# GpSimd waits for its scatters to land before it ends its part of a block

## What is computed

```
x = x + 0.5 * ffn(layernorm(x))       # top-1 of 8 experts, silu(a) * g @ w2, times its probability
x = x + mamba(layernorm(x))           # conv, selective scan over 1024 steps, gate, out, layer norm
x = x + 0.5 * ffn(layernorm(x))
```

## Time and profile before

| | us |
|---|---|
| three runs | 426.71, 425.19, 426.67 |
| median | 426.67 |
| span of the profiled execution, first to last instruction | 421.5 |
| PE busy | 373.5 (89%) |
| DVE busy | 309.6 (73%) |
| ACT busy | 261.8 (62%) |
| GpSimd busy | 260.0 (62%) |

### The profile page before, as it was taken

The page is one execution under the profiler, slowest core; times in us unless marked ns, Lnnn a source line. Parts: engine busy times, 40 slices in busy tenths (PEclk is TensorE's granted clock), DMA queues, the critical chain, the costliest instruction groups (busy, mean ns, idle before and its releaser), DMA issues.

```text
span 421.5 us, 8456 instructions
## 1 busy us (share of the span) xinstructions
PE 373.5 (89%) x2962; PEld 339.5 (81%) x2962; DVE 309.6 (73%) x475; ACT 261.8 (62%) x508; POOL 260.0 (62%) x190
## 2 busy tenths in 40 slices
PE   7398999996799988999999899999998298999994
PEld 7297988896664377899998789999898297998994
DVE  2844454472699699999999999999979845544561
ACT  2314333341397999999999999999645414433330
POOL 7054666654001009999999999999960054666643
PEclk9679999999699999999999999999999689999999
DMA  6928592210300168654444344434337321121110
GB/s 197 346 61 253 131 406 64 47 33 32 101 0 4 30 165 20 150 158 132 126 158 155 125 126 166 144 130 130 108 117 285 90 40 41 38 47 46 40 39 25
DMA packets 42730, 47.47 MB, mean 113 GB/s; under 512 B 13313, under 2 KB 34370, under 8 KB 42178
## 3 DMA queue, kind: packets, MB, share of 16 engines
q1 hardware_dynamic: 37634, 39.72, 31.7%
q0 software_dynamic: 2944, 6.13, 6.1%
q10 hardware_dynamic: 2112, 1.08, 1.2%
HBM read 37.38 MB, written 9.54 MB: 111 GB/s over the span
## 4 chain that ended last, share of the span: by engine, by line
ACT 35%; PE 16%; DVE 15%; POOL 3%; issue 2%; another core or an unknown queue 1%; DMA 1%; POOLq 0%; DVEq 0%; ACTq 0%
ACT phase L1050 16%; ACT phase L1060 14%; PE psum L660 9%; PE psum L672 5%; DVE xc L1287 4%; DVE phase L966 3%; POOL w_sb L885 2%; DVE x_tok L1012 1%; ACT dt L920 1%; DVE xc L1283 1%; PE psum L1151 1%; PE psum L1183 1%; POOL phase L373 1%; DMA phase<-token_rows,token_row 1%
## 5 line engine op out<-in xcount | busy, mean ns | idle before, releaser
L885 POOL TENSOR_TENSOR w_sb<-phase,w_sb 128x1024 f32<-128x1024 f32 x62 | 144.7, 2378 | 0.0
L966 DVE TENSOR_TENSOR_SCAN phase<-phase,psum 128x1024 f32<-128x1024 f32 x64 | 142.1, 2272 | 3.0 <-PE psum L1133 2.3
L660 PE MATMUL psum<-phase 128*128 128x128 f32 x736 | 92.1, 277 | 4.6 <-ACT phase L559 2.9
L660 PEld LDWEIGHTS psum<-phase 128*128 128x128 f32 x736 | 86.5, 192 | 6.8 <-ACT phase L559 3.5
L373 POOL DMA_INDIRECT phase<-token_rows,token_row x46 | 47.2, 1027 | 55.3 <-DVE token_row L475 25.8
L1050 ACT ACTIVATE phase<-dtxT,B_cols 128x256 f32<-128x256 f32 x192 | 79.9, 495 | 0.2
L1151 PE MATMUL psum<-ident,w_sb 128*128 128x128 f32 x512 | 67.5, 276 | 3.3 <-DVE silu_z L959 0.9
L1060 ACT ACTIVATE phase<-dt,neg_A 128x1024 f32<-128x1024 f32 x64 | 69.6, 1136 | 0.0
L496 DVE TENSOR_TENSOR phase<-phase,psum 128x512 f32<-128x512 f32 x46 | 31.4, 684 | 45.1 <-PE psum L660 21.8
L1151 PEld LDWEIGHTS psum<-ident,w_sb 128*128 128x128 f32 x512 | 56.5, 141 | 8.7 <-POOL w_sb L885 6.9
L1124 PE MATMUL psum<-ident,phase 128*128 128x128 f32 x384 | 55.6, 276 | 1.5 <-DVE phase L966 0.6
(11 more groups left out here) (180 smaller groups left out, 401.5 us busy)
## 6 DMA issues: line engine op xcount, KB each, us to landing
w_sb<-c_rows SPq DMA_DIRECT2D x32, 512.0 KB, 3.9
w_sb<-ffn_w SPq DMA_DIRECT2D x16, 512.0 KB, 7.3
B_diag<-dt SPq DMA_DIRECT2D x4, 1024.0 KB
phase<-B_diag SPq DMA_DIRECT2D x32, 128.0 KB, 3.8
w_sb<-ffn_w SPq DMA_DIRECT2D x8, 256.0 KB, 7.8
token_rows<-x_tok SPq DMA_DIRECT2D x4, 264.0 KB, 4.9
token_rows<-x_tok ACTq DMA_DIRECT2D x4, 264.0 KB, 6.0
x_tok<-attn_x SPq DMA_DIRECT2D x4, 256.0 KB, 4.1
```

Source lines behind the costliest of these rows:

```text
L660: last = nc.tensor.matmul(psum[:, 2 * k + part, c * P:(c + 1) * P], w1_tile[:, t % W1_RING, part * F + c * P:part * F + (c + 1) * P], xsT_ ...
L885: nc.gpsimd.tensor_tensor(hC[:, k % HC_RING, :], H[:, k % H_RING, :], C_sb[:, j % C_RING, :], ALU.mult).then_inc(M["hC_ready"], 1)
L966: nc.vector.tensor_tensor_scan(H[:, k % H_RING, :], dA[:, k % DECAY_RING, :], dBx_bank[k % SLOTS], 0.0, ALU.mult, ALU.add).then_inc(M["sca ...
```

## The change

The function that waits for the scatters takes any engine, and GpSimd calls it behind its last scatter, in both expert layers. SyncE's own wait stays.

```diff
-        def wait_scattered(sp, f):
+        def wait_scattered(engine, f):
             for k in range(YS_RING):
-                sp.wait_ge(f["ys_stored"][k], f["ys_before"][k] + 16 * ((SLOT_TILES - 1 - k) // YS_RING + 1))
+                engine.wait_ge(f["ys_stored"][k], f["ys_before"][k] + 16 * ((SLOT_TILES - 1 - k) // YS_RING + 1))
...
                 scatter(t)
+            wait_scattered(pool, f)
```

## The result

The change makes the kernel slower: 428.84 us in the median of 8 runs (427.28 to 436.19) against 425.12 us in 8 runs of the kernel before (423.92 to 426.71). The ratio is 1.0067 with a 95% interval of 1.0036 to 1.0099, + 2.8 us by the ratio and + 3.7 us by the medians; forecast were + 3.3 us.

A forecast was written before the change was run, and what follows sets the result against it. TensorE was busy 89% of 421.5 us, but the change touches the block ends, where GpSimd's DRAIN sets the program's last 2.4 us. 1.57 + 1.75 = 3.3 us on 426.67 gives 430.0 us, range 424.4 to 431.0.

The forecast's parts named there:

- The DRAIN, started later: At both block ends: GpSimd's DRAIN, pushed behind the new waits, still takes 3.8 us as work of fixed length; chance 0.62.
- The rule that was weighed: At GpSimd's DRAIN: if it only waits for an idle engine, it would be over at once, giving 424.6 us.
- The turning point: At the program's end: a DRAIN under 2.2 us behind the wait would make the forecast wrong in sign.
- End of the program: At the second block's end: DRAIN ends at 422.8 in place of 421.25, nothing hides it, + 1.57 us.
- End of the first block: Release at 109.7 in place of 107.95, + 1.75 us, which the second block passes on in full.
- The starts that were named: Expected trace times: GpSimd's DRAIN at 105.7 (first block) and near 420.7 (program's end), VectorE's L820 near 109.8 us.
- TensorE's clock: Behind the first block's release: the clock's rise moves with the restart, the chain there runs through VectorE, so nothing added.
- The absolute time: Whole kernel: 426.67 us before plus 3.3 us gives 430.0 us.
- The reading of the 5.2 us: Outside the profiled span: the runs' median exceeds the span by 5.2 us, left as they are by the change.
- The first: Rival on GpSimd's DRAIN: it waits for outstanding DMAs and costs next to nothing once landed; 424.6 us, chance 0.17.
- the second: Rival on GpSimd's DRAIN: the 3.8 us start by themselves behind the last scatter, both releases stay; 426.7 us, chance 0.14.
- the third: Rival on the first block's end: its delay is taken up in the second block, + 1.57 us alone; 428.2 us, chance 0.07.

The follow-up runs named there:

- e5: Kernel before plus one GpSimd DRAIN inside each expert layer, behind tile 7 in the first and tile 15 in the second; one run for the trace, 424.75 us.
- e6: Kernel before plus a second GpSimd DRAIN right behind each layer's last scatter, ahead of the block's own; one run for the trace, 422.18 us.
- e8: Changed kernel, waits in both layers, plus an early GpSimd DRAIN behind tile 15 in both; ratio 0.9952 to the kernel before, 420.69 us.
- e7: Kernel before plus one early GpSimd DRAIN behind tile 15 of the second expert layer alone; ratio 0.9970, 421.59 us.
- e2: Changed kernel with GpSimd's wait in the first expert layer only; ratio 1.0033 to the kernel before, + 1.4 us.
- e1: Changed kernel with GpSimd's wait in the second expert layer only; ratio 1.0039 to the kernel before, + 1.7 us.

## Why the prediction was right

*The DRAIN, started later.* This step decided the sign, and held: 3.83 and 3.81 us behind the wait, 3.8 forecast. The reason given held in its first half (work of a length, begun when GpSimd gets to it, not a wait for data) and left open which work; e5, e6 and e8 showed it to be a price for each DMA issued since the last DRAIN. That it doesn't follow the landing is true only with many DMAs: with 7 to 24 of them it does, with half of its price still behind. Here there was luck in the argument. The two equal lengths in spite of unequal landings, on which it rested, came about because half of the price of 46 DMAs, 1.91 us, was just over the later landing, 1.80 us; with 40 DMAs the first block's DRAIN would have followed its landing by the fitted rule. The rule that was weighed, that a drain waits for the engine to be fully idle (the Trainium skill, "PSUM — Partial Sum Buffer", section "Engine vs sequencer instructions"), tells nothing of this price. The turning point that the prediction named, a DRAIN under 2.2 us behind the wait, holds only against a DRAIN that was long without the wait too. With few DMAs both are short, and the wait still costs: e8's takes 0.62 us behind the wait, and its end comes 2.45 us behind the last scatter, against 1.82 us in e7 without the wait.

*End of the program.* + 1.57 us forecast, 5.63 - 4.05 = 1.58 measured. The 0.15 us from wait to DRAIN, taken from SyncE, was right.

*End of the first block.* + 1.75 us forecast, 6.19 - 4.37 = 1.82 measured, and passed on: e2 alone costs 1.4 us of time (0.2 to 2.6). The starts that were named (105.7, 420.7, 109.8) came at 104.6, 422.7 and 108.75, because in this execution the stretch up to the first layer's last scatter took 1.1 us less and the one behind the release 3.0 us more; the distances from the last scatters are the ones forecast.

*TensorE's clock,* for which nothing was added. The profiled execution after does lose something there: in the stretch that was at 0.95 it is still at 0.50, 1.2 GHz, and its chain of waits runs through the preliminary tiles, 6.50 us for what took 5.79:

```profile
112.00:114.00 2.00, 2.00 (x11) 2.00 (x10) 1.63 (x9) 0.71 (x3) 0.00 (x0) 0.50 0.00 0
...
108.75 6.50 PE psum L335 x32
```

So the step "the chain runs through VectorE there" didn't hold in this execution. But the kernel e1, whose first block ends as before (release at 107.9), shows the same late clock; its stretch:

```profile
112.00:114.00 2.00, 2.00 (x13) 2.00 (x12) 1.86 (x9) 1.26 (x3) 0.00 (x0) 0.57 0.00 0
```

From the release to ScalarE's second table load it is 15.07 us before, 15.55 after, 15.32 in e2, but 15.64 in e1 and 15.71 in e7, whose first blocks end as before, and 15.06 in e8, which has both waits. So the later clock, worth 0.2 to 0.6 us, comes in some executions, with the waits and without.

*The absolute time.* 430.0 us forecast, 428.84 measured, 1.2 us less. What missed was the base: 426.67 us was the median of three runs, and eight runs of the same kernel have 425.12, 1.55 us less; the difference, + 3.7 us by the medians in place of + 3.3, takes 0.4 of that back. The reading of the 5.2 us as what lies "ahead of the first and behind the last instruction" was wrong too, but it stood on both sides and cancels. In the experiments each timed run comes with its own span, and time less span is 1.7 to 1.8 us in all of them. By that the profiled execution took an estimated 421.5 + 1.75 = 423.2 us, a fast one: the kernel before spreads from 423.8 to 428.6 us over 35 runs.

*The rivals.* The first (cheap once landed) and the second (work that runs by itself) would have given a DRAIN of 0.2 us, or of 1.8 and 2.2 us; both are refuted by the two lengths. Against the third (delay taken up in the second block) stands e2, by an interval that begins at + 0.2 us, and its trace.

## What to carry to other kernels

Where a block ends right behind indirect DMAs of GpSimd, look for its DRAIN: the chain of waits doesn't show it, the listing by line does, and a span that is longer than the chain's end is the hint. Here it costs 0.083 us for each indirect DMA since the DRAIN before, or more where the last landing is late, and a wait put ahead of it adds to it: 1.6 us at the program's end with 46 DMAs, 0.6 with 7. Leave the DRAIN out where another engine waits for the landing anyway (whether it guards something else in another kernel, no run here shows), or place one DRAIN earlier beside other work, so that the last has few DMAs to account for. The place matters: behind tile 15 no delay showed, behind tile 7 of the first layer the last tile came some 4 us later in the one trace of it.

## What the runs showed of the hardware that was not expected

The DRAIN of GpSimd: 0.041 us with no DMA since the last, 0.62 with 7 landed, 3.25 with 39, 3.81 to 3.84 with 46, landed or not, each from the DRAIN's start or from the end of the scatter that it waits for; where the landing comes later than half of the price, it ends 0.33 (7 DMAs) to 1.03 us (24) behind the landing. In one trace a load issued right behind a block's start took 4.7 us to its landing, against 2.8 before, and another took 2.3 us to issue beside a fetch of instructions; the cause of neither is shown.
